# A recurrence beside attention: a quarter of its units moved behind attention, and the end of a sequence laid over the next projections

## The chip, the cores and the metric

The kernel runs on one core of one Trainium2 chip. Its time is the device time of one execution in microseconds (us). One launch computes two layers for 8 sequences of 512 tokens with 256 features, all in float32.

## The reference

Two layers, each `x = x + s * silu(g)`, with `s` from a recurrent branch and `g` from a second branch, both of the layer-normed input. The first layer (a gated scan, and experts chosen per token) is not touched. The second one is:

```python
# recurrent branch (16 channels a head, 16 heads; x is the normed input)
dx = shift(x) - x;  lerpx = x + dx * xw
r, k, v, g = [(x + dx * lora(lerpx, ...)) @ W.T for each]      # lora: l + tanh(z @ a.T) @ b.T
w = exp(-exp(lora(x + dx * lora(lerpx, d...), d...)))
for t in range(T):                                             # state: 16 x 16 a head
    y[t] = r[t] @ (state + u * outer(k[t], v[t]))
    state = w[t] * state + outer(k[t], v[t])
s = (silu(g) * layernorm_per_head(y)) @ oW.T
# second branch
x2 = xn + causal_attention(rmsnorm(xn))                        # 16 heads, rotated queries, one shared latent key
f = x2 + shared_expert(rmsnorm(x2)) + top2_of_8_experts(rmsnorm(x2))
out = x + s * silu(f)
```

## The kernel before

Three phases follow each other; the change is in the third, `phase_c`, which takes the sequences one by one (B = 8) in a loop on every engine. Each engine has its own instruction list; the order in a list is the order of the code, and engines meet only at semaphores. Nothing plans the order, it is written out.

One sequence has these stages.

- Projections (TensorE L1080 `product`, in the order of the table `PRE`): la (the low-rank inputs), lb (their outputs, one pair for each of d, r, k, v, g), pr (the projections), then xb, ckv and q0 to q7. VectorE makes each mix from lb (L1509), GpSimd adds x to it (L1742), TensorE projects it. VectorE and GpSimd rotate ckv and the eight q (L1523, L1524, L1747, L1749). ScalarE copies r, k, v, g out of PSUM and makes w (L1343, L1359).
- Attention, 32 steps of two heads and 128 queries each (8 head pairs, 4 query tiles, step i has tile i % 4), written in one loop per engine. TensorE: `scores` (L1124, L1127), then `turn_probs` for step i-2 (L1139); `weigh_values` (L1165) and `spread_inverse` (L1156) every 8 steps. VectorE: `highest` (the row maxima, L1545). ScalarE: `exp` (L1372) and `keep` (L1381), the copy of the transposed probabilities. Scores are two steps ahead (LAG = 2).
- The recurrence runs beside attention in 32 units (one unit: 8 heads x 16 channels of k on the partitions, for one channel of v). SP copies one channel of v over 16 partitions a head (L1048, 256 KB, four buffers), VectorE multiplies by k (`outer`, L1558) and scans over time with w (`scan`, L1565), GpSimd sets the first column of the state (L1753) and multiplies with r (`product`, L1758), TensorE sums over channels in bank 4 for four units at a time (`reduce_state`, L1147). One unit stands in each step of VectorE's loop: `highest(i)`, `scan(i)`, `outer(i + 1)`. Sixteen units make one half of y (`read_out`, L1570).
- Behind attention (TensorE L1249 `result` for all that follows): mean0, wo0, wo1 (the output of attention), mean1, var0; VectorE adds wo to xn (L1598), subtracts the means (L1593); ScalarE squares (L1405); the root (L1779), the scaled rows xb (L1605), their transposes xc0, xc1 (L1086), the copy of the first (L1614), var1, and the gate.
- Experts, e = 0 to 8: TensorE `up(e)`, `down(e - 1)`; ScalarE silu (L1400), VectorE `hidden` (L1660) and four accumulations (L1703). Between two experts VectorE does one step each of the two halves of y's normalisation (reciprocal L1666, L1670, L1674, L1679) and of the next sequence's head (gate, sum, statistics, norm, rms, lerp; L1439 to L1481).
- End of a sequence: the gate matmuls o0 and o1 (8 matmuls), silu of the accumulator (L1424), product (L1709) and sum (L1713), store. The next sequence's first projection waits for PSUM reads of this one, and the loop jumps here.

PSUM has eight banks of 128 x 512 float32. `Outputs` gives each result of the tables `PRE` and `POST` its bank in turn, all eight, and TensorE waits before it writes for the reader of the result that had the bank before.

## Time and profile before

| | us |
|---|---|
| three runs | 2812.10, 2814.43, 2822.92 (median 2814.43) |
| profiled execution | 2821.07 |
| its span, first to last instruction | 2818.8 |
| TensorE (PE) busy | 2332.4 (83%), 9640 records |
| VectorE (DVE) busy | 1768.5 (63%) |
| GpSimd (POOL) busy | 1029.7 (37%) |
| ScalarE (ACT) busy | 924.0 (33%) |
| mean granted TensorE clock | 0.887 |

Busy shares are means over stages that have different limits, so they say little here; phase_c has one period per sequence, and the windows of one period are what to read. A group of instructions is shown by its line, engine and operation, with its count, busy time and mean duration, and the idle time of the engine just ahead of it with what ended that (`<-`). A float32 matmul leaves two records. "issue" is idle time for which the profile shows no releaser. PEclk is the granted clock as a share of 2.4 GHz; 0.5 is 1.2 GHz.

### The profile page before, as it was taken

The page shows a single profiled execution, that of the slowest core. Times are in us where ns is not written, and L with a number is a line of the kernel's source. Part 1 is how long each engine was busy: PE and PEld are TensorE (multiplying, and loading weights), DVE is VectorE, ACT ScalarE, POOL GpSimd, SP SyncE. Part 2 cuts the span into 40 slices and gives each one's busy share as a digit, 9 for nine tenths or more (in the row PEclk, how much of TensorE's full clock was granted, in tenths as well). Part 3 has the DMA queues.
Part 4 walks back from the last instruction along what each step waited for, and adds up shares of the span by engine and source line. Part 5 has one row for each costly group of instructions (what it writes and reads, how often), then busy time and mean ns, then how long its engine had stood idle before and what let it go on. Part 6 is the DMA issues. An engine that isn't in the chain of part 4 may idle for free.

```text
span 2818.8 us, 36206 instructions
## 1 busy us (share of the span) xinstructions
PE 2332.4 (83%) x9640; PEld 1276.8 (45%) x9641; DVE 1768.5 (63%) x2977; ACT 924.0 (33%) x2467; POOL 1029.7 (37%) x986
## 2 busy tenths in 40 slices
PE   7887599996877987798789778978888797789778
PEld 3443366664434533443454345434534443454345
DVE  5777344443278658666855785477748566855777
ACT  2333123321235224412532352234225413522352
POOL 2113200001166146506622661265155416622661
PEclk9998799998778997898789888979997898889799
DMA  4341401003043014202410440143024203401430
GB/s 138 112 143 63 152 26 30 28 28 98 4 55 62 23 24 72 57 9 33 77 34 9 50 70 23 21 57 67 9 29 76 47 9 41 78 24 19 55 71 16
DMA packets 100043, 143.57 MB, mean 51 GB/s; under 512 B 7953, under 2 KB 61841, under 8 KB 99857
## 3 DMA queue, kind: packets, MB, share of 16 engines
q1 hardware_dynamic: 92370, 128.18, 23.1%
q0 software_dynamic: 3264, 8.93, 1.1%
q10 hardware_dynamic: 4224, 4.19, 0.4%
q8 instruction: 91, 1.49, 0.2%
q14 instruction: 94, 0.77, 0.1%
HBM read 50.94 MB, written 23.24 MB: 26 GB/s over the span
## 4 chain that ended last, share of the span: by engine, by line
issue 29%; PE 16%; DMA 11%; DVE 9%; POOL 8%; ACT 2%; DVEq 0%; POOLq 0%; ACTq 0%
DMA arena<-arena 11%; PE bank L1249 8%; DVE arena L1565 3%; POOL arena L1742 3%; POOL arena L1747 2%; DVE arena L1545 2%; PE bank L1139 2%; DVE arena L1558 2%; PE bank L1124 2%; PE bank L1165 2%; POOL arena L1749 1%; ACT arena L1372 1%; PE bank L1156 1%; ACT arena L1381 1%; PE bank L1147 1%
## 5 line engine op out<-in xcount | busy, mean ns | idle before, releaser
L1249 PE MATMUL bank<-arena 128*128 128x256 f32 (+2 forms) x1728 | 531.8, 468 | 6.4 <-DVE arena L1574 6.2
L1758 POOL TENSOR_TENSOR arena<-arena 128x512 f32<-128x512 f32 x256 | 370.1, 1446 | 291.7 <-issue 151.8
L1080 PE MATMUL bank<-arena 128*128 128x512 f32 (+2 forms) x896 | 423.9, 619 | 46.1 <-issue 18.6
L1372 ACT ACTIVATE arena<-bank,arena 128x128 f32<-128x128 f32 (+3 forms) x512 | 267.0, 526 | 545.5 <-DVE arena L1545 488.7
L1139 PE MATMUL bank<-arena 128*128 128x128 f32 x1280 | 257.4, 340 | 208.9 <-ACT arena L1381 207.5
L1249 PEld LDWEIGHTS bank<-arena 128*128 128x128 f32 x1728 | 331.8, 201 | 196.9 <-issue 153.3
L1565 DVE TENSOR_TENSOR_SCAN arena<-arena 128x512 f32<-128x512 f32 x256 | 375.8, 1468 | 0.0
L1139 PEld LDWEIGHTS bank<-arena 128*128 128x128 f32 x1280 | 186.2, 175 | 249.0 <-ACT arena L1372 213.5
L1080 PEld LDWEIGHTS bank<-arena 128*128 128x128 f32 (+2 forms) x896 | 159.7, 189 | 296.3 <-issue 255.4
L1124 PE MATMUL bank<-arena 64*128 64x128 f32 (+3 forms) x1024 | 257.3, 586 | 43.9 <-DVE arena L1524 26.9
L1558 DVE TENSOR_TENSOR arena<-arena 128x512 f32<-128x512 f32 x256 | 209.1, 817 | 77.0 <-DMA arena<-arena 76.7
L1545 DVE TENSOR_REDUCE arena<-bank 128x2 f32<-128x256 f32 (+3 forms) x256 | 209.3, 817 | 53.3 <-PE bank L1127 52.9
L263 PE MATMUL bank<-arena 128*128 128x512 f32 x384 | 189.4, 647 | 34.3 <-DVE arena L417 18.1
L1381 ACT ACTIVATE arena<-bank 128x128 f32<-128x128 f32 (+3 forms) x512 | 196.7, 441 | 11.6 <-PE bank L1139 11.4
L1742 POOL TENSOR_TENSOR arena<-arena 128x512 f32<-128x512 f32 x80 | 99.3, 1268 | 250.8 <-DVE arena L1509 250.8
L1753 POOL COPY arena<-arena 128x1 f32<-128x1 f32 x256 | 164.1, 641 | 0.0
L1124 PEld LDWEIGHTS bank<-arena 64*128 64x128 f32 x1024 | 95.7, 229 | 141.2 <-issue 95.8
L1509 DVE SCALAR_TENSOR_TENSOR arena<-bank,arena 128x512 f32<-128x512 f32 x80 | 60.2, 753 | 157.8 <-PE bank L1080 152.7
L696 PE MATMUL bank<-arena 128*128 x624 | 147.3, 388 | 1.3 <-ACT arena L730 1.3
L676 PE MATMUL bank<-arena 128*128 x312 | 142.1, 598 | 1.2 <-DVE arena L771 1.2
L817 POOL TENSOR_TENSOR arena<-arena 128x1 f32<-128x1 f32 x39 | 21.2, 543 | 330.6 <-DVE arena L763 330.6
L263 PEld LDWEIGHTS bank<-arena 128*128 128x128 f32 x384 | 76.0, 204 | 130.8 <-issue 90.2
(189 smaller groups left out, 2887.4 us busy)
## 6 DMA issues: line engine op xcount, KB each, us to landing
arena<-arena SPq DMA_DIRECT2D x256, 256.0 KB
arena<-in_L_attn_h SPq DMA_DIRECT2D x17, 512.0 KB, 3.6
arena<-in_W1T SPq DMA_DIRECT2D x8, 1024.0 KB, 5.8
arena<-in_W2T SPq DMA_DIRECT2D x8, 1024.0 KB, 8.8
sorted_rows<-arena SPq DMA_DIRECT2D x42, 128.5 KB, 9.0
arena<-sorted_rows SPq DMA_DIRECT2D x40, 128.5 KB, 2.1
gate_rows<-arena SPq DMA_DIRECT2D x39, 128.0 KB, 1.7
arena<-s_rows SPq DMA_DIRECT2D x9, 512.0 KB, 4.6
```

Of the source, the lines that this page charges most:

```text
L263: last = nc.tensor.matmul(bank[s + q][:, :], gru_w[layer][:, k, q * D + m * P:q * D + (m + 1) * P], src[:, k, :], start=(k == 0), stop=(k ...
L1080: last = nc.tensor.matmul(dst[0:rows, 0:width], w, x, start=(n == 0), stop=(n == len(pairs) - 1))
L1124: nc.tensor.matmul(bank[2 * (i % LAG) + half][:, 0:n], qT[rows, p, qt * P:(qt + 1) * P], ckvT[rows, 0:n], start=True, stop=False)
L1139: last = nc.tensor.transpose(bank[5 + half][:, kt * P:(kt + 1) * P], probs[s % PROBS][:, kt * P:(kt + 1) * P], ident)
L1249: last = nc.tensor.matmul(dst[o], w, x, start=first, stop=last_one)
L1372: nc.scalar.activation(probs[s % PROBS][:, 0:n], bank[2 * (i % LAG) + half][:, 0:n], ACT.Exp, bias=neg_max[:, s:s + 1], accum_out=row_sum[ ...
L1381: nc.scalar.activation(turned[h % HGROUP][:, 0:qt + 1, qt * P:(qt + 1) * P], bank[5 + half][:, 0:(qt + 1) * P].rearrange("p (k c) -> p k c ...
L1545: nc.vector.tensor_reduce(neg_max[:, 2 * i:2 * i + 2], psum[:, at:at + 1024].rearrange("p (h k) -> p h k", h=2)[:, :, 0:n], X, ALU.max, ne ...
L1558: nc.vector.tensor_tensor(kv[n % 2], copies[n % COPIES], proj["k"][:, n // HD, :], ALU.mult).then_inc(kv_done, 1)
L1565: nc.vector.tensor_tensor_scan(state[n % 2][:, 1:T + 1], proj["w"][:, m, :], kv[n % 2], VEC["init"][:, m * HD + j:m * HD + j + 1], ALU.mul ...
L1742: nc.gpsimd.tensor_tensor(mix[n % 2][:, m, :], mix[n % 2][:, m, :], xnT[:, m, :], ALU.add).then_inc(mixed, 1)
L1758: nc.gpsimd.tensor_tensor(prods[n % PRODS], state[n % 2][:, 0:T], proj["r"][:, m, :], ALU.mult).then_inc(prod_done, 1)
```

## The change

- Each of the 32 units is no longer tied to a step. Unit 0 runs in the projections (between the rotations of q5 and q6), units 1 to 23 in those steps of attention with i % 4 != 3, units 24 and 25 behind the last maximum, 26 and 27 between the steps up to the gate, 28 to 31 between experts 0 to 3.
- So the second half of y is complete only in the experts. Its mean and variance, and the reductions, use bank 4 alone (`LAST_BANK`), which both tables leave out: each now turns over seven banks. Its reciprocal, scale, affine and gate, the gate matmuls (`gates`), product, sum and store run in the next sequence's projections.
- The loop on each engine is turned: `before_attention(0)`, then seven times `attention(b)` and `before_attention(b + 1)`, then `attention(B - 1)` and an end of its own. The head that was made for a ninth sequence is gone.
- State has four buffers, not two. Its first column is no longer written by GpSimd but by a small DMA of SP per unit. The load of the next sequence stands within SP's copies, after the 28th.
- xb, xbT, acc and y have memory of their own; the wait for the store moves from the first rotation to the first accumulation.
- Ahead of the last weighing of values TensorE does mean0 and six of the 16 wo matmuls. Scores no longer wait for the last rotated q as a whole.

The core of the diff:

```diff
+STATES = 4
+UNIT_STEP = [i for i in range(PSTEPS) if i % NT != NT - 1]
+EARLY = len(UNIT_STEP)
+PRE_BANKS = [3, 5, 6, 7, 0, 1, 2]
+POST_BANKS = [2, 0, 1, 3, 5, 6, 7]
+LAST_BANK = 4
 # SP
+            def first_column(b, n):
+                if n >= STATES:
+                    sp.wait_ge(prod_done, UNITS * b + n - STATES + 1)
+                sp.dma_start(state[n % STATES][:, 0:1], VEC["init"][:, n:n + 1]).then_inc(init_in[n % STATES], 16)
+            def sequence(b, last):
                 sp.wait_ge(a_read, pre.read(b, "pr_v1"))
+                for n in range(STATES):
+                    first_column(b, n)
                 for n in range(UNITS):
+                    copy_value(b, n)
+                    if n > STATES:
+                        first_column(b, n - 1)
+                    if n == EARLY + COPIES and not last:
+                        sp.wait_ge(pv_mm, GROUPS * b + 2 * GROUPS)
+                        load_sequence(b + 1)
+                first_column(b, UNITS - 1)
+                store_sequence(b)
 # TensorE, projections
                 project(b, "r")
                 lora_b(b, "v", "v", th[1])
+                if ended is not None:
+                    gates(ended, 0)
                 project(b, "k")
                 lora_b(b, "g", "g", th[1])
+                if ended is not None:
+                    gates(ended, 1)
 # TensorE, attention
+                    if i == PSTEPS + LAG:
+                        pe.wait_ge(y_read, 2 * b + 1)
+                        pe.wait_ge(s_exp, STEPS * b + STEPS)
+                        result("mean0", [(full, mean_m, y[:, 0, :], True, True)], bank[post.bank("mean0")])
+                        pe.wait_ge(y_out, GROUPS * b + GROUPS - 1)
+                        wo(0, 0, range(GROUPS - 1))
+                        wo(1, 0, range(GROUPS - 1))
 # TensorE, experts
+                    if e == 2:
+                        reduce_state(b, EARLY // 4)
+                    elif e == 6:
+                        reduce_state(b, EARLY // 4 + 1)
+                    elif e == ME:
+                        mean_last(b)
                     if e:
                         down(e - 1)
-                pe.wait_ge(o_done, 2 * b + 2)
-                for half in range(2):
-                    by_tokens(f"o{half}", ...)
+                var_last(b)
 # ScalarE, end of the experts
                 nc.scalar.activation(acc, acc, ACT.Silu).then_inc(f_done, 1)
+                root_last(b)
 # VectorE
+            def unit(b, n):
+                scan(b, n)
+                if n + 1 < UNITS:
+                    outer(b, n + 1)
 # VectorE, projections, after the mixes of x
+                        if x == "d":
+                            ln_inv(ended, 1)
+                        elif x == "r":
+                            ln_scale(ended, 1)
+                            ln_affine(ended, 1)
+                            ln_gate(ended, 1)
+                        elif x == "v":
+                            gate_rows(ended, 0)
+                        elif x == "g":
+                            gate_rows(ended, 1)
+                            residual(ended)
+                        if name == "q5":
+                            outer(b, 0)
+                            v.wait_ge(w_step, 2 * b + 2)
+                            scan(b, 0)
+                            outer(b, 1)
 # VectorE, attention
-                    if i < PSTEPS:
-                        scan(i)
-                    if i + 1 < PSTEPS:
-                        outer(i + 1)
+                    if i in UNIT_STEP and i > 0:
+                        unit(b, UNIT_STEP.index(i))
+                    if i == PSTEPS:
+                        unit(b, EARLY)
+                    if i == PSTEPS + 2:
+                        unit(b, EARLY + 1)
+                        center()
 # VectorE, between the experts
+                    if e < 4:
+                        unit(b, EARLY + 4 + e)
+                    elif e == 4:
+                        ln_inv(b, 0)
+                    elif e == 5:
+                        read_out(b, 1)
+                        ln_scale(b, 0)
+                    elif e == 6:
+                        ln_affine(b, 0)
+                    elif e == 7:
+                        center_last(b)
+                        ln_gate(b, 0)
 # GpSimd, the product of a unit
-                    nc.gpsimd.tensor_copy(state[n % 2][:, 0:1], VEC["init"][:, m * HD + j:m * HD + j + 1]).then_inc(init_set, 1)
-                    g.wait_ge(init_set, UNITS * b + (n + 1))
+                    g.wait_ge(init_in[n % STATES], 16 * (UNITS // STATES) * b + 16 * (n // STATES + 1))
                     g.wait_ge(scan_done, UNITS * b + (n + 1))
```

`mean_last`, `var_last` and `gates` are TensorE's matmuls in bank 4; `center_last` and `root_last` are VectorE's subtraction and ScalarE's root for the second half of y.

## Rows read from the trace of the kernel before

**Rows 1.** Windows of one sequence (length; busy us and records an engine; clock, DMA).
```profile
2040.00:2103.20 63.20, 55.12 (x128) 21.99 (x128) 26.08 (x46) 13.01 (x21) 29.77 (x26) 0.97 0.18 26
2103.20:2211.40 108.20, 82.77 (x514) 43.75 (x514) 94.42 (x103) 55.44 (x185) 72.78 (x69) 0.81 0.43 69
2211.40:2223.50 12.10, 9.05 (x62) 4.78 (x62) 2.13 (x4) 4.68 (x11) 3.43 (x3) 0.72 0.04 11
2223.50:2238.30 14.80, 10.72 (x47) 8.10 (x48) 6.50 (x12) 1.81 (x8) 4.76 (x7) 1.00 0.18 63
2238.30:2299.40 61.10, 58.84 (x188) 35.71 (x186) 44.47 (x99) 14.20 (x27) 4.66 (x5) 0.92 0.03 10
```

**Rows 2.** Groups of instructions by line, of attention (2103.2 to 2211.4).
```profile
L1565 DVE TENSOR_TENSOR_SCAN arena<-arena 128x512 f32<-128x512 f32 x32 | 47.8, 1493 | 0.0
L1372 ACT ACTIVATE arena<-bank,arena 128x128 f32<-128x128 f32 (+3 forms) x62 | 32.0, 521 | 65.0 <-DVE arena L1545 58.0 <-PE bank L1139 6.9
L1545 DVE TENSOR_REDUCE arena<-bank 128x2 f32<-128x256 f32 (+3 forms) x32 | 26.2, 818 | 6.1 <-PE bank L1127 6.0
L1558 DVE TENSOR_TENSOR arena<-arena 128x512 f32<-128x512 f32 x32 | 25.6, 800 | 7.7 <-DMA arena<-arena 7.7
L1753 POOL COPY arena<-arena 128x1 f32<-128x1 f32 x32 | 20.5, 640 | 0.0
```

**Rows 3.** Windows: first four copies of v, then three parts of attention.
```profile
2074.00:2098.50 24.50, 23.44 (x66) 10.67 (x65) 13.07 (x26) 6.01 (x10) 12.81 (x12) 1.00 0.39 43
2104.50:2126.50 22.00, 16.25 (x72) 8.03 (x71) 20.46 (x21) 10.77 (x38) 16.64 (x16) 0.61 0.44 51
2126.50:2146.00 19.50, 14.90 (x88) 7.19 (x87) 11.48 (x15) 7.63 (x25) 8.93 (x11) 0.65 0.46 75
2146.00:2204.50 58.50, 45.23 (x321) 25.78 (x320) 54.28 (x60) 33.47 (x110) 40.79 (x37) 0.91 0.47 81
```

**Rows 4.** Instructions of two lines in attention (ns: least, median, most).
```profile
L1565 DVE TENSOR_TENSOR_SCAN arena<-arena x32: 1194/1277/1964, 2104.8 to 2211.3; 128x512 f32<-128x512 f32 x32
...
L1558 DVE TENSOR_TENSOR arena<-arena x32: 660/667/1509, 2103.0 to 2209.6; 128x512 f32<-128x512 f32 x32
```

**Rows 5.** DMA issues of the whole execution (count, KB each, us to landing).
```profile
arena<-in_gate_b SPq DMA_DIRECT2D x1, 4.0 KB, 6.5
```

**Rows 6.** Timeline behind the last maximum (start, us, engine, line; idle before).
```profile
2224.23 9.75 PE L1249 MATMUL bank<-arena 128*128 128x512 f32 x38 [0.78 <-DVE arena L1574]
...
2238.03 0.75 DVE L1614 TENSOR_SCALAR arena<-bank,arena 128x512 f32<-128x512 f32 x1
```

**Rows 7.** Timeline of the experts, from TensorE's, ScalarE's and VectorE's lists.
```profile
2238.27 52.59 PE L1249 MATMUL bank<-arena 128*128 128x512 f32 x154
...
2239.22 1.28 ACT L1410 ACT_TABLE_LOAD   x1
...
2255.53 3.34 DVE L1666 RECIPROCAL arena<-arena 128x512 f32<-128x512 f32 x1
...
2285.97 0.69 DVE L1660 TENSOR_TENSOR arena<-arena,bank 128x512 f32<-128x512 f32 x1 [2.34 <-ACT arena L1400]
```

**Rows 8.** TensorE's timeline from one sequence's last expert to the next scores.
```profile
2033.33 5.35 PE L1249 MATMUL bank<-arena 128*128 128x256 f32 x24
2040.12 0.69 PE L1080 MATMUL bank<-arena 128*128 128x512 f32 x1 [1.45 <-DVE arena L1703]
2042.90 6.83 PE L1080 MATMUL bank<-arena 128*128 128x512 f32 x11 [2.08 <-issue]
...
2054.95 24.11 PE L1080 MATMUL bank<-arena 128*64 128x512 f32 x52 [0.83 <-POOL arena L1742]
...
2103.27 0.49 PE L1124 MATMUL bank<-arena 64*128 64x128 f32 x4 [3.36 <-DVE arena L1524]
```

**Rows 9.** VectorE's timeline at the end of the last sequence.
```profile
2810.22 1.41 DVE L1703 SCALAR_TENSOR_TENSOR arena<-bank,arena 128x256 f32<-128x256 f32 x4
...
2814.17 1.23 DVE L1713 TENSOR_TENSOR arena<-arena 128x1024 f32<-128x1024 f32 x1
```

More of the change, by code:

```diff
@@ L942, in phase_c @@
         kv = [mem.take(T) for _ in range(2)]
-        state = [mem.take(T + 1) for _ in range(2)]
+        state = [mem.take(T + 1) for _ in range(STATES)]
         probs_at = mem.at
@@ L1230, in _, with attention, result, by_tokens @@
                         product(b, name, [(spread, bonus[:, i, :])])
-                pe.wait_ge(a_read, pre.read(b, "lat"))
-                pe.wait_ge(v_read, pre.read(b, "q7"))
+            def attention(b, final):
+                full = slice(None), slice(0, T)
+                def result(name, pairs, dst):
+                    begin(b, name, post, post_read)
+                    for n, (o, w, x, first, last_one) in enumerate(pairs):
+                        last = nc.tensor.matmul(dst[o], w, x, start=first, stop=last_one)
+                    last.then_inc(made2, 1)
+                def by_tokens(name, tiles, lhs, rhs, n):
+                    result(name, [((slice(None), slice((i % 2) * D, (i % 2 + 1) * D)), lhs(i, c), rhs(c), c == 0, c == n - 1)
+                                  for i in tiles for c in range(n)], bank[post.bank(name)])
+                def wo(half, odd, groups):
+                    dst = bank[post.bank(f"wo{half}")]
+                    i = 2 * half + odd
+                    for c in groups:
+                        last = nc.tensor.matmul(dst[:, odd * D:(odd + 1) * D], yT[c][:, i * P:(i + 1) * P], wo_w[:, c, :],
+                                                start=(c == 0), stop=(c == GROUPS - 1))
+                    if odd:
+                        last.then_inc(made2, 1)
                 for i in range(PSTEPS + LAG + 3):
@@ L1325, in _ @@
             act.sem_inc(a_read, 1)
[L1326 removed]
+            act.sem_inc(a_read2, 1)
             act.sem_inc(stored, 16)
```

438 lines of the change are left out of this document (242 added, 196 removed).

## The prediction

> **What bounds the kernel now.** I read the windows of one sequence first. The eight sequences of the last phase repeat every 259.4 us: 63.2 us of projections, 108.2 us of attention with the recurrence beside it, 12.1 us until its last value, 14.8 us up to the gate, 61.1 us of experts with the gated output [rows 1]. TensorE is busy for all but about 2 us of the experts; in attention VectorE leads, 94.4 of 108.2 us. What is worth looking for in each stretch is the engine without gaps.
>
> The groups of attention [rows 2] say what VectorE does there: 32 scans (mean 1493 ns), 32 outer products (800 ns), 32 row maxima (818 ns). ScalarE's exponentials wait 58.0 us for the maxima: VectorE works in order, maximum, scan, outer product, so each exponential queues behind a unit of the recurrence. VectorE itself waits 7.7 us for copies of v and 6.0 us for scores.
>
> The windows inside attention [rows 3] show three rates. In the first 22.0 us VectorE is busy 20.5 at a granted clock of 0.61, in the next 19.5 us only 11.5, in the last 58.5 us 54.3. The middle one is the DMA's: the copies move 51, 75 and 81 GB/s in the three, for 256 KB each 5.1, 3.5 and 3.2 us a copy, against 3.4 us a step (108.2 / 32).
>
> **The change, part by part.** Durations are those of one execution of 2821.1 us (span 2818.8, 2.3 around it); the median of the runs shown is 2814.4, so the result is taken 6.6 lower at the end.
>
> *Attention, eight times.* Of 32 units (a scan and an outer product) unit 0 goes into the projections, 24 to 31 go behind the last maximum; 23 stay. Of VectorE's 94.4 us, 26.2 are maxima and about 5 small work, so a unit costs (94.4 - 31) / 32 = 2.0 us, nine units 18, and 76 us of VectorE's work is left. Idle now: 13.8 us. If that stayed, less the 7.7 of DMA wait, the stretch would take 82 us, 26 less. But the others are near then: per four steps TensorE needs 8.4 us at full clock (82.8 x 0.81 / 8), ScalarE 6.9 (55.4 / 8), VectorE 9.5 after and 11.8 before. Three engines in order, with scores two steps ahead, should leave more gaps; I take 16 us: 76 + 16 = 92. The low end of the gain: the first 22 us at half clock give nothing, the DMA's gap stays, and the other 58.5 us shrink in the ratio 9.5 to 11.8 but lose a fifth of it: 9. I take -16, between -9 and -26, nearer VectorE's rows than TensorE's, since its gaps are the smaller. Eight times: -128.
>
> GpSimd's 32 copies of the first column (20.5 us a sequence) go too [rows 2]. They go at nothing: GpSimd is busy 72.8 of 108.2 us. The 32 DMAs in their place stand in SP's order between the copies of v, and each waits for the product four units back. No row shows a copy of 4 bytes a partition; the nearest, 4 KB, landed 6.5 us after issue in a crowded queue [rows 5]. Four units are 15 us, so a product waits nothing, or 6.5 us once if the queue is full; below nothing it can't go but by a shorter GpSimd. I take 0.
>
> Scans take 1194 to 1964 ns and outer products 660 to 1509 [rows 4]. The Trainium skill's page "SBUF — State Buffer", section "SBUF: two separate sides", says that a VectorE operation with two inputs in SBUF and a GpSimd operation that reads there lock each other out for a whole instruction. The spread of those two rows agrees. By that rule the units carried into the experts, whose products go with them, would all come at the long price: the second rival below.
>
> *Behind the last maximum, eight times.* Units 24 and 25 fall where VectorE is busy 2.1 of 12.1 us [rows 1]: hidden. On TensorE mean0 (0.85) and six of the 16 wo matmuls (0.43 each) move ahead of the last weighing: 3.4 us, of which 0.7 fills a wait, so +2.7; behind it 3.6 less stands in the block of 38 records in 9.75 us [rows 6]: -0.9. Unit 26 stands between the second residual sum and the root; ScalarE's squares there take 1.5 us, the unit 2.0 and some wait: +0.7. Unit 27 stands in the chain from the scaled rows to the copy of their transpose (2238.03) [rows 6], that the gate waits for: +1.7. Together +1.5, between -1 and +4: +12.
>
> *Experts, eight times.* TensorE has 154 records in 52.6 us, almost without a gap [rows 7]. It gets two reductions of 1.04 us and the mean of the second half, 0.85: +2.9, not hidden. VectorE gets units 28 to 31 and loses one reciprocal of 3.34 us and 1.9 us of small steps. An expert takes 5.17 us of TensorE and 2.3 of VectorE's own two steps, so 2.8 are free; experts 1 to 4 bring 3.2 to 3.4. It is some 1.3 us late at the next sequence's normalisation, for which it already waits 2.34 us ahead of L1660 [rows 7], and TensorE after it: +1.5. Together +4.4, between +2.9 and +8: +35.
>
> *From the last expert to the next scores, seven times.* I count from the last expert's 8 records, 2033.33 + 1.8 = 2035.1, to 2103.3 [rows 8]: 68.2 us, of which 19.8 lie before la_dd (2054.95) and 45.0 up to the last projection. Gone: the gate matmuls ahead (3.5), the wait for the last accumulate behind them, and the pause of 2.08 us after the first record, which I read as the loop's jump. It comes back at the head of attention, in place of the 3.36 us for the last rotated q [rows 8]. Then la_dd comes at 17.1: lerp 3.3 (its chain is 0.7 longer), two thirds of the first projections wait for the accumulate until 5.0, then 11.3 of la, tanh, lora and mix as now, and 0.4 for two more table loads of 1.28 us [rows 7]; 0.4 less since the tanh comes earlier. Behind it 45.0, the eight gate matmuls 3.5, less 1.9 of gaps that they fill, and 1.6 because the reciprocal (3.34) stands between the d and r mixes and project r waits for r: 48.2. Then the jump 2.1, and 0.4 for units 0 and 1 among the rotations. In sum 67.8: -0.4, between -3 and +4: -2.
>
> *The end, once.* The last sequence's second half has nothing to run beside: root with load 1.9, reciprocal 3.3, three steps 1.9, gates 3, product and sum 1.9, waits 1.8: 13.8, where 3.8 stand now (2811.6 to 2815.4) [rows 9]. The dropped ninth head gives 2.5 back: +7.5, between +4 and +12.
>
> Sum: -128 + 12 + 35 - 2 + 7.5 = -75.5: 2746, by the median 2740 us.
>
> **Rivals.** *The copies set the pace.* Four of them queued at once moved 43 GB/s over 24.5 us [rows 3], about 5.3 us a copy. For it: the DMA share is 0.44 to 0.47 in all of attention and no higher where the rate is, as if full. Needed after: 23 copies in 92 us, 4.0 each. If they stay at 5.3, the lead of six copies lasts to about unit 14; ten more units then cost 1.4 each: the gain of attention is 2 and not 16: -16 + 52.5 = +36, 2851. It decides where a copy takes over 4.0 us to the end. Against: the rate rises from 51 to 81 within a sequence, and the demand falls.
>
> *The experts pay it back.* The units come there at the long price of rows 4, 3.5 us and not 2.0, since GpSimd's products run beside: 6 us a sequence, all of it TensorE's: 48, so 2788. For it: GpSimd has 4.7 us of work in that stretch now and gets about 6 more. Against: VectorE's result for the next matmul is up to 3.8 us ahead, which takes part of it.
>
> *TensorE is attention's true bound.* Clock 0.81, busy 82.8 of 108.2 [rows 1]: the gain is 7, the costs the same: -56 + 52.5: 2811, no change. Against: 58.5 us with VectorE 93% busy at clock 0.91 [rows 3].
>
> *It overlaps better*: idle stays near 6 us, 82 us of attention: 80 less, 2660.
>
> **Chances.** The forecast with its own 2700 to 2785: 0.60; the experts pay back 0.12; TensorE 0.09; the copies 0.09; better overlap 0.10. A difference under 0.5% (14 us; 2800 to 2828) can't be told from none here. Faster are the forecast, the payback and the better one, 0.82, less 0.03 for the payback's tail: 0.79; same 0.09; slower, the copies and that tail, 0.12. The range leaves out the end of the better case and most of the copies: 2675 to 2815.
>
> **What would show it.** A period near 250 us. From the first score to the last maximum near 92 us with VectorE busy near 76, and little wait for copies; if that wait is over 15 us a sequence, the copies rule. The experts near 57 us for 52.6, with longer gaps before L1660's successor. The first projections without the 2.08 us pause, the reciprocal behind the d mixes, five table loads a sequence for three. I am wrong if attention stays above 100 us, or if TensorE's gaps in the experts pass 8 us a sequence.

## The result and the profile after

The changed kernel takes 2926.36 us (median of 4 runs, 2916.67 to 2935.75) against 2813.26 for the kernel before: a ratio of 1.040, interval 1.035 to 1.046, some 113 us slower. The forecast was 2740, faster. The profiled execution has a span of 2933.9 us; it had 2818.8.

The windows of one sequence, the same five stretches as in [rows 1] and with the same columns:
```profile
2092.60:2159.80 67.20, 62.46 (x146) 25.81 (x147) 34.64 (x52) 15.50 (x23) 27.49 (x22) 0.92 0.17 25
2159.80:2277.50 117.70, 80.85 (x499) 44.48 (x498) 77.02 (x94) 55.63 (x185) 48.03 (x34) 0.81 0.45 49
2277.50:2292.20 14.70, 11.38 (x76) 6.88 (x76) 5.59 (x7) 4.68 (x11) 5.64 (x5) 0.88 0.48 54
2292.20:2305.40 13.20, 7.44 (x31) 5.67 (x30) 8.61 (x14) 3.78 (x11) 4.49 (x6) 0.83 0.61 132
2305.40:2364.50 59.10, 57.05 (x186) 32.76 (x186) 43.44 (x95) 10.83 (x23) 11.49 (x10) 0.92 0.07 14
```
The whole loss of attention is in the second row: 117.7 us where 108.2 stood, although VectorE's work fell from 94.4 to 77.0 as forecast. All engines have gaps now, and the DMA moves 49 GB/s instead of 69 at the same share. The row above it is longer too (67.2 against 63.2), the row of the experts is shorter because the gated output has gone from it into the next sequence's first row.

The groups of the page that answer to [rows 2], for the whole execution (busy and mean ns, idle before them):
```profile
L1885 POOL TENSOR_TENSOR arena<-arena 128x512 f32<-128x512 f32 x256 | 361.6, 1413 | 794.8 <-DVE arena L1639 446.3
...
L1619 DVE TENSOR_REDUCE arena<-bank 128x2 f32<-128x256 f32 (+3 forms) x256 | 206.5, 820 | 160.3 <-PE bank L1147 142.8
L1632 DVE TENSOR_TENSOR arena<-arena 128x512 f32<-128x512 f32 x256 | 199.7, 780 | 168.4 <-DMA arena<-arena 168.2
```
The outer products (L1632) wait 168.2 us for copies of v, where the page of before has 76.7. The products (L1885) wait 341.8 us for the small DMAs (L1059), as the third view below says. It and the two ahead of it give the durations of SyncE's issues in ns (least, median, most): first the copies of the kernel before, then the copies and the small DMAs of the one after.
```profile
L1048 SPq DMA_DIRECT2D arena<-arena x256: 647/1464/4796, 768.5 to 2717.0; - x128
```
```profile
L1052 SPq DMA_DIRECT2D arena<-arena x256: 647/4312/4777, 768.8 to 2849.8; - x128
```
```profile
L1059 SPq DMA_DIRECT2D arena<-arena x256: 521/577/5014, 766.1 to 2855.6; - x128
...
  POOL arena L1885: 341.8, 108
```
A copy's issue took 1.5 us in the median, up to 4.8, and takes 4.3 in the median now. SyncE's own list, in attention (start, duration):
```profile
2182.29 0.58 SPq L1059 DMA_DIRECT2D arena<-arena  x1
2183.27 4.10 SPq L1052 DMA_DIRECT2D arena<-arena  x1
2187.42 0.58 SPq L1059 DMA_DIRECT2D arena<-arena  x1
2188.11 4.23 SPq L1052 DMA_DIRECT2D arena<-arena  x1
```
Copy and small DMA take turns almost without a pause: 4.0 to 4.5 us, then 0.6 to 0.9, about 5.1 us a pair. They do so from 2183.3 on, to the end of the stretch, 94 of its 117.7 us. SyncE, which no row ahead of the prediction times, holds back the rest there.

To compare stages over all sequences I took from VectorE's timeline the first and last row maximum, the last scaled value and the accumulates of the experts. Mean of the first seven sequences, us:

| stretch | before | after | forecast of the difference |
|---|---|---|---|
| first to last row maximum | 109.6 | 108.9 | -16 |
| to the last value | 12.8 | 15.4 | +1.5 with the next row |
| to the first accumulate | 29.0 | 27.9 | |
| first to last accumulate | 44.6 | 48.8 | +4.4 |
| to the next first maximum | 64.6 | 73.1 | -0.4 |
| period | 260.7 | 274.0 | -10.5 |

The table counts from maximum to maximum, the forecast from the first score. By the forecast's count attention went from 108.1 to 117.9 us in the sequence of the rows, and in the mean from 110.7 to 118.0 (+7.3): the first maximum now comes 9.8 us after the first score in that sequence, where it came 1.2 after. From the last accumulate to the next first score the mean went from 63.4 to 63.9 (+0.5). The experts and the stretch behind the last maximum came out as forecast, and the way to the next scores within the range given for it; attention did not.

### The profile page after: what moved, and what is told of

Read it like the earlier page. It is cut to its first block, busy times and chain, and to the rows that moved or that the text cites. A ratio compares the mean times of both kernels' runs of the same rounds, so it can differ in the third digit from the quotient of the medians.

```text
span 2933.9 us, 35683 instructions
## 1 busy us (share of the span) xinstructions
PE 2356.5 (80%) x9632; PEld 1285.1 (44%) x9633; DVE 1736.5 (59%) x2951; ACT 932.3 (32%) x2466; POOL 892.0 (30%) x722
## 3 DMA queue, kind: packets, MB, share of 16 engines
q1 hardware_dynamic: 128178, 127.28, 27.6%
## 4 chain that ended last, share of the span: by engine, by line
PE 30%; DMA 19%; issue 10%; DVE 9%; POOL 3%; ACT 3%; SPq 1%; DVEq 0%; ACTq 0%; POOLq 0%
DMA arena<-arena 19%; PE bank L1272 13%; PE bank L1098 10%; PE bank L1161 1%; DVE arena L1619 1%; DVE arena L1632 1%; DVE arena L1639 1%; PE bank L1216 1%; PE bank L1144 1%; ACT arena L1442 1%; POOL arena L1872 1%; DVE arena L1825 1%; POOL arena L1874 1%; DVE arena L1689 1%; PE bank L1171 1%
## 5 line engine op out<-in xcount | busy, mean ns | idle before, releaser
L1885 POOL TENSOR_TENSOR arena<-arena 128x512 f32<-128x512 f32 x256 | 361.6, 1413 | 794.8 <-DVE arena L1639 446.3
L1098 PE MATMUL bank<-arena 128*128 128x512 f32 (+2 forms) x896 | 448.3, 649 | 39.4 <-ACT arena L1403 22.2
L1272 PE MATMUL bank<-arena 128*128 128x512 f32 (+2 forms) x1312 | 447.0, 496 | 6.3 <-ACT arena L1407 6.3
L1639 DVE TENSOR_TENSOR_SCAN arena<-arena 128x512 f32<-128x512 f32 x256 | 341.5, 1334 | 23.3 <-issue 22.9
L1272 PEld LDWEIGHTS bank<-arena 128*128 128x128 f32 x1312 | 256.1, 209 | 192.0 <-issue 155.3
L1161 PEld LDWEIGHTS bank<-arena 128*128 128x128 f32 x1280 | 188.0, 177 | 282.6 <-ACT arena L1442 254.0
L1144 PE MATMUL bank<-arena 64*128 64x128 f32 (+3 forms) x1024 | 245.0, 561 | 70.4 <-ACT arena L1442 69.1
L1632 DVE TENSOR_TENSOR arena<-arena 128x512 f32<-128x512 f32 x256 | 199.7, 780 | 168.4 <-DMA arena<-arena 168.2
L1098 PEld LDWEIGHTS bank<-arena 128*128 128x128 f32 (+2 forms) x896 | 167.4, 197 | 301.1 <-issue 236.2
L1867 POOL TENSOR_TENSOR arena<-arena 128x512 f32<-128x512 f32 x80 | 103.2, 1307 | 224.0 <-DVE arena L1664 224.0
L263 PEld LDWEIGHTS bank<-arena 128*128 128x128 f32 x384 | 75.1, 202 | 129.6 <-issue 88.9
L1403 ACT ACTIVATE arena<-bank 128x512 f32<-128x512 f32 (+1 forms) x96 | 55.6, 595 | 233.9 <-PE bank L1098 233.8
L696 PEld LDWEIGHTS bank<-arena 128*128 128x128 f32 x624 | 116.0, 191 | 29.9 <-issue 14.3
```

Source lines behind the costliest of these rows:

```text
L263: last = nc.tensor.matmul(bank[s + q][:, :], gru_w[layer][:, k, q * D + m * P:q * D + (m + 1) * P], src[:, k, :], start=(k == 0), stop=(k ...
L696: last = nc.tensor.matmul(out_bank[u % 2][:, 0:D], hT[:, c, :], w2s[:, bass.ds((E - 1) * FC * D + c * D - e * (FC * D), D)], start=False, ...
L1098: last = nc.tensor.matmul(dst[0:rows, 0:width], w, x, start=(n == 0), stop=(n == len(pairs) - 1))
L1144: nc.tensor.matmul(bank[2 * (i % LAG) + half][:, 0:n], qT[rows, p, qt * P:(qt + 1) * P], ckvT[rows, 0:n], start=True, stop=False)
L1161: last = nc.tensor.transpose(bank[5 + half][:, kt * P:(kt + 1) * P], probs[s % PROBS][:, kt * P:(kt + 1) * P], ident)
L1272: last = nc.tensor.matmul(dst[o], w, x, start=first, stop=last_one)
```

## The experiments

Every kernel was compared with runs of the kernel before on the same chip (medians 2810 to 2815); the ratios carry the comparisons, and 0.01 is 28 us. "After" and "before" below are the two kernels.

**Who writes the first column.** GpSimd's copy of 128 x 1, as before, in place of SyncE's DMAs; the four state tiles and the moved units stay.
```
-                for n in range(STATES):
-                    first_column(b, n)
...
+                    nc.gpsimd.tensor_copy(state[n % STATES][:, 0:1], VEC["init"][:, n:n + 1]).then_inc(init_set, 1)
```


> The changed kernel, with the first column of the state written by GpSimd again (four buffers stay) and SP's 32 small DMAs a sequence gone. Theory: the small DMAs hold the copies of v (SP issues each only after a product, in order with the copies, and a product waits for them 341.8 us in all), so products no longer wait for a DMA, the outer product's wait of 168 us falls under 60, and attention goes from 118 to about 100 us a sequence: 2780 to 2810 us. Rival: the copies themselves are slow because they queue on the DMA engines, whatever stands between them: the outer product's wait stays over 130 us and the time at 2890 or more.

Measured: 2836.0 us, ratio 1.007 (1.004 to 1.010). 94 of the 113 us are gone with the small DMAs, but it is not the 2780 to 2810 that I expected. The outer products wait 0.0 us for copies, and the median issue of a copy is near the least one:
```profile
L1052 SPq DMA_DIRECT2D arena<-arena x256: 647/662/4796, 766.3 to 2750.1; - x128
```

The reverse, the small DMAs put into the kernel before (with four state tiles):
```
+                    if n > STATES:
+                        first_column(b, n - 1)
```


> The kernel before, with only this part of the change: four state buffers, and the first column of each unit by a small DMA of SP in the order of the change, not by GpSimd. Theory (the small DMAs hold the copies): attention with all 32 units becomes bound by the copies at about 5 us each, 150 us for 108: over 3000 us, at the least 2900. Rival (the copies are slow for another reason, such as the pace at which units are asked for): within 30 us of the kernel before.

Measured: 3120.6 us, ratio 1.108 (1.102 to 1.114). Attention alone takes 148.2 us from the first to the last maximum, where it took 109.6: with 32 units it needs some 29 pairs of issue at 5.1 us. So the small DMAs cost more in the kernel with more units in attention, 309 us, and the two runs show the same pace.

**Why they cost: a wait, a DMA or its packets.** On top of GpSimd's column, first SyncE's 28 waits without the DMAs, then the 32 DMAs without the waits, into memory that nobody reads, then the same DMAs with one row of 32 bytes in place of 128 rows of 4.
```
+            def column_wait(b, n):
+                if n >= STATES:
+                    sp.wait_ge(prod_done, UNITS * b + n - STATES + 1)
...
```


> The kernel after, with the first column written by GpSimd as in the pool-column run (2836 us), but SyncE still waits at the 28 old places of each sequence for the product four units back; no small DMA is issued. If it is SyncE's order (a copy held behind a wait for a product) that costs the 90 us between 2836 and 2926, this run comes near 2926. If it is the DMAs themselves (their issue and their place in the rings beside the copies), it stays near 2836. I expect 2840, within 2825 to 2860: the product four units back is some 12 us old when its place in the order comes.

Measured: 2841.8 us, ratio 1.009 (1.006 to 1.012), against 1.007 without them: the waits cost nothing that can be told.
```
+            def unread_column(b, n):
...
+                sp.dma_start(nobody[:, n:n + 1], VEC["init"][:, n:n + 1]).then_inc(unread, 16)
```


> The kernel after, with the first column written by GpSimd, but SyncE issues a DMA of the same shape (128 partitions, 4 bytes each) at each of the 32 old places, into memory that nobody reads, with no wait for a product ahead of it. If the DMAs themselves cost the time (they fill the queue in which the copies stand, so each copy lands later), this comes to 2890 to 2930 with VectorE's outer products waiting for copies again. If the wait of a product for its column was the cost, or SyncE's waits, it stays near 2836. I expect 2905.

Measured: 2922.3 us, ratio 1.039 (1.035 to 1.042), the time of after. No product waits for these DMAs, so it isn't the products' wait either. (SyncE itself waits once a sequence, ahead of the last one, until the others have landed.)
```
-                sp.dma_start(nobody[:, n:n + 1], VEC["init"][:, n:n + 1]).then_inc(unread, 16)
+                sp.dma_start(nobody[0:1, 8 * n:8 * n + 8], VEC["init"][0:1, 0:8]).then_inc(unread, 16)
```


> As the run with the 32 unread DMAs a sequence (2922 us), but each moves one row of 32 bytes in one partition, not 4 bytes in each of 128. If the number of small transfers inside a DMA costs the time (128 each, beside the copies' own 128), this comes near the kernel without small DMAs, 2836 to 2850. If each DMA costs by its issue on SyncE or its place in the queue, whatever is in it, it stays near 2922. I expect 2850.

Measured: 2925.3 us, ratio 1.039 (1.035 to 1.042). My expectation was wrong: a DMA of one row costs what one of 128 rows costs. Its issue on SyncE is no shorter (least, median, most ns):
```profile
L1061 SPq DMA_DIRECT2D arena<-arena x256: 670/722/4712, 768.1 to 2851.1; - x128
```
So with either content it is the further DMA in the order that costs. Nor are its packets the cost: the queue moved 95410 packets in this execution and 128178 in the one ahead of it.

**The same DMAs from another engine.** ScalarE issues them behind each pair of exponentials.
```
                         exp(2 * i + 1)
...
+                        act.dma_start(nobody[:, i:i + 1], VEC["init"][:, i:i + 1]).then_inc(unread, 16)
```


> The changed kernel with GpSimd's column (2836 us) and 32 unread DMAs of 128 x 4 bytes a sequence, now issued by ScalarE behind each pair of exponentials, in a queue of their own. If the cost in SyncE's queue (2922) was its order of issue, where copy and small DMA take turns at 5.1 us a pair, the copies run free here, and only ScalarE's issue costs: 2840 to 2860. If the small DMAs hold up the engines wherever they are queued, 2900 or more. I expect 2850.

Measured: 3018.6 us, ratio 1.072 (1.067 to 1.077), wrong again. The copies do run free (their issue, first row, and VectorE waits 0.0 us for them), but the small DMAs now hold up ScalarE (second row), and the exponentials stand behind it:
```profile
L1054 SPq DMA_DIRECT2D arena<-arena x256: 647/662/4789, 766.3 to 2934.8; - x128
```
```profile
L1462 ACTq DMA_DIRECT2D arena<-arena x256: 513/1072/4279, 799.5 to 2912.6; - x128
```
An issue that takes 0.5 us at least takes 1.07 in the median and up to 4.28 while copies are under way from the other queue. Of the 183 us over 2836, 19.3 are the run's own doing: ahead of its last DMA of a sequence ScalarE waits for the landing of the others. The page "DMA: Bandwidth & Descriptors" of the Trainium skill says, in "Issuing engines are not separate DMA queues", that DMAs of all issuers run on the same engines, and that issuing from several saves only the issuer's time. The trace fits the first part; the issuer's time, which that text calls usually small beside the DMA itself, is here most of the cost.

**Why attention had nothing to give.** In the kernel before, scan, outer product and product of every fourth unit cut to 8 columns, with nothing put elsewhere:
```
+def wide_of(n):
+    return 8 if n % 4 == 3 else T
```


> The kernel before with scan, outer product and product of every fourth unit (8 of 32, at the steps that the changed kernel leaves free) cut to 8 of 512 columns: that part of the recurrence isn't computed; the copies, waits and every other instruction stay. It prices alone what attention gains when VectorE has eight units less, with nothing put elsewhere. By the forecast's term (16 us a sequence for nine units) 14 us a sequence go: 2700. If attention is bound by the copies' rate or by TensorE and ScalarE behind one another, 3 to 7 us a sequence: 2755 to 2790. I expect 2740.

Measured: 2810.7 us, ratio 1.000 (0.998 to 1.003). A quarter of the recurrence's work on VectorE is gone and no time with it, where I expected 2740. This is the run that the forecast's main term needed and did not have. Its row of attention, counted from the first maximum (columns as in [rows 1]; before has 107.0 us by this count), and its groups of maxima and outer products in the whole execution:
```profile
2083.20:2189.80 106.60, 81.61 (x506) 44.37 (x504) 78.71 (x103) 55.88 (x185) 55.21 (x68) 0.81 0.44 70
```
```profile
L1551 DVE TENSOR_REDUCE arena<-bank 128x2 f32<-128x256 f32 (+3 forms) x256 | 209.7, 819 | 126.3 <-PE bank L1133 126.2
...
L1564 DVE TENSOR_TENSOR arena<-arena 128x512 f32<-128x512 f32 (+1 forms) x256 | 184.2, 720 | 103.6 <-DMA arena<-arena 103.0
```
VectorE is busy 78.7 us of 106.6, about what it is in the changed kernel. What it lost in work it now waits: 126.2 us for scores in the execution, where before had 52.9, and 103.0 for copies, where it had 76.7.

Copies of v cut to 8 of 512 columns, alone and with the thin units:
```
-                    sp.dma_start(copies[n % COPIES],
+                    sp.dma_start(copies[n % COPIES][:, 0:8],
```


> The kernel before with every copy of v cut to its first 8 of 512 columns, in the same 128 rows; outer products read what lay in the rest, so the recurrence isn't computed rightly, but every instruction stays. It takes the load off the DMA queue. VectorE's 76.7 us of waits for copies go; if the copies pace attention, 60 us or more come back: 2750 or less. If TensorE's chain is as near a bound, half or less of it: 2780 to 2800. I expect 2775.

> The kernel before with thin copies and, besides, the 8 units of 32 cut to 8 columns on VectorE and GpSimd (what both leave out is as in those two runs). If VectorE was the bound once the copies are out of the way, this run lies 60 us or more below the thin copies alone. If the chain scores, maximum, exponential, transpose is the bound, it lies within 25 us of it. I expect 20 below it.

Measured: 2757.3 us, ratio 0.979 (0.972 to 0.986), and 2738.8, ratio 0.974 (0.969 to 0.979). Their rows of attention:
```profile
2067.40:2170.60 103.20, 81.14 (x506) 44.83 (x504) 93.40 (x103) 56.02 (x185) 74.10 (x68) 0.82 0.02 2
```
```profile
2044.80:2145.10 100.30, 79.95 (x506) 43.07 (x504) 76.93 (x103) 56.00 (x185) 56.30 (x68) 0.83 0.02 2
```
Without the copies' load attention takes 103.2 us, and eight units less then bring 3 more (16 to 19 us in the execution). In the last row VectorE is busy 76.9 us of 100.3 and the DMA moves 2 GB/s, and still the stretch is 100 us long. Neither VectorE's work nor the copies fill it; that scores, maxima, exponentials and transposes behind one another do is what is left to argue, since 24 of 32 units still stand between the maxima and no run takes them out. The forecast's 92, counted from the first score, lay below it.

**The loops' jumps.** In after, VectorE's loop begins anew between the last rotated q and the first maximum. Its seven iterations written out, in after, in after with GpSimd's column, and as the control in before:
```
-            with v.Fori(0, B - 1) as b:
+            for b in range(B - 1):
```


> The changed kernel, with VectorE's seven loop iterations written out one behind the other, so VectorE has no jump between projections and attention. Theory: the pauses of 2.9 us before and 3.8 us behind the first two maxima of a sequence are the jump, now exposed at the head of attention: about 5 us a sequence back, 2880 to 2895 us. Rival: the copies set the pace of attention and swallow it: 2915 to 2930, the pauses gone all the same. A third way: the pauses stay, being no jump.

> The kernel after with GpSimd's column and VectorE's seven iterations written out instead of a loop. Theory: at the head of attention VectorE pauses 2.9 and 3.8 us where its loop begins anew, on the path to the first exponentials, in seven sequences; without the pauses 3 to 6 us a sequence go: 2795 to 2815. Rival: the first scores wait for the rotated q and the steps behind are TensorE's, so it stays at 2836.

> The kernel before with VectorE's loop over the eight sequences written out, nothing else. It is the control for the unrolled run of the changed kernel (2801 us): there the loop's jump stood at the head of attention, here it stands between the last accumulate and the first projections. If the jump is hidden there, 2811 and no change, and then the moved units with GpSimd's column are worth 10 us in all. If this run gains as much as the changed kernel did by it (34 us, 2780), the move itself is a loss of 20. I expect 2807.

Measured: 2918.8 us, ratio 1.039 (1.033 to 1.045); 2801.5, ratio 0.996 (0.994 to 0.999); 2790.1, ratio 0.991 (0.988 to 0.995). With the small DMAs the jump is hidden behind them. Without them it brings 30 us in the changed kernel and, against my expectation, 25 in the kernel before. In both changed kernels the pauses of VectorE at the head of attention are gone. All four loops (TensorE, ScalarE, VectorE, GpSimd) written out:

> The changed kernel with GpSimd's column and the seven iterations of the last phase written out on TensorE, ScalarE, VectorE and GpSimd (with VectorE's alone: 2801 us). TensorE's jump stands at the head of attention, where its first scores wait for the rotated q as well. If the jump of TensorE was the later of the two, 8 to 15 us go: 2788. If it was hidden behind the rotations, 2801 stays. I expect 2793.

> The kernel before with the eight iterations of the last phase written out on TensorE, ScalarE, VectorE and GpSimd (VectorE's alone: 2790 us). TensorE's pause of 2.08 us at the first projection goes too: by the forecast's reading of it 8 to 17 us less, 2775 to 2782. If VectorE's jump was the later one, 2790 stays. I expect 2778. Against the changed kernel with the same two mendings (2797) it then shows the move to lose some 19 us.

Measured: 2796.8 us, ratio 0.995 (0.993 to 0.998), and 2767.9, ratio 0.984 (0.980 to 0.988). The last is the fastest kernel of this study that computes everything, 5.4% below after and 1.6% below before, and has nothing of the change in it. Against one another the two show the rest of the change, without small DMAs and without jumps: 0.0115, some 32 us slower. I call them the clean pair, and the rest "the move".

**Where the moved units cost.** Unit 0 out of the rotations and into step 0 of attention, in after and in the unrolled kernel with GpSimd's column:
```
-                        if name == "q5":
-                            outer(b, 0)
...
-                    if i in UNIT_STEP and i > 0:
+                    if i in UNIT_STEP:
```


> The changed kernel, with unit 0 (outer product, scan, second outer product) no longer between the rotations of q5 and q6: the first outer product comes behind the last rotation, the unit in step 0 behind the first maximum. Theory: the first maximum comes about 3.5 us earlier and attention's end follows it, 20 to 30 us in all: 2895 to 2905. Rival: the recurrence loses its head start and the copies set the pace, so nothing or a loss of up to 30: 2920 to 2955.

> The kernel after with GpSimd's column, VectorE's loop written out, and the inserted unit 0 and outer products moved from between the rotations of q5 and q6 to behind the last rotation and into step 0 of attention. Theory: the inserted work of 5.3 us holds back q6 and q7 and with them the first scores, so the sequence starts earlier than in the unrolled run and the unit is hidden in step 0: 10 to 30 us less than that run: 2780 to 2800, the first below the kernel before. Rival: attention's first four steps are already VectorE's, and the unit costs there what it cost ahead: the same as the unrolled run.

Measured: 2936.4 us, ratio 1.044 (1.038 to 1.051), and 2824.0, ratio 1.002 (1.000 to 1.004), both against my expectation, the second 16 to 23 us slower than with the unit among the rotations. The unit costs more in attention's first step: 99.7 us between first and last maximum, where 95.1 stood, and only 1.3 less ahead of it. Units 24 to 31 cut to 8 columns:
```
+def wide_of(n):
+    return 8 if n >= 24 else T
```


> The changed kernel with GpSimd's column and VectorE's loop written out (2801 us), and scan, outer product and product of units 24 to 31 cut to 8 of 512 columns: that part of the recurrence isn't computed. It prices what the eight units cost behind the last maximum and in the experts' stretch. By the forecast's terms (1.5 and 1.5 us a sequence of VectorE's lateness) some 20 us go: 2781. If the units cost more there, with GpSimd's products beside VectorE's steps, 40 us or more: 2760 or below. I expect 2775.

Measured: 2780.8 us, ratio 0.987 (0.984 to 0.991): 26 us less by the ratios, 21 by the medians; the expectation was 20 to 26. The traces put it ahead of the experts, not in them: from the last value to the first accumulate 27.1 us became 24.7 in the mean, and the accumulates themselves went from 48.4 to 48.0. Unit 27 behind the copy of the transposed rows instead of ahead of it:
```
-                unit(b, EARLY + 3)
                 v.wait_ge(made2, post.made(b, "xc0"))
...
+                unit(b, EARLY + 3)
```


> The changed kernel with GpSimd's column and all four loops written out (2797 us), and unit 27 moved from ahead of the copy of the transposed rows, which the gate waits for, to behind it. By the forecast's term of 1.7 us a sequence 13 us go, of which VectorE's later routing gives some back: 2788. If the unit only moves the delay from the gate to the routing, 2797 stays.

Measured: 2799.6 us, ratio 0.994 (0.991 to 0.997), no difference from 0.995. The copy comes 0.5 us earlier there, and the routing begins 16.8 us behind the last value in both: at this place the unit held nothing up.

## Why the prediction was wrong

By the ratios the 113 us are: 94 for the small DMAs; 32 for the move itself; and -13, since the jumps cost 33 us in the changed kernel and 45 in the one before.

The 32 come about so in the clean pair's traces, by the forecast's count and as means of seven sequences: attention -7.0, up to the first accumulate +1.6, the accumulates +4.3, from there to the next scores +4.9, so +3.8 a sequence and not -10.5; the rest is the last sequence. Attention gained less than half of the 16, and the way to the next scores, put at -0.4, took most of that back.

**The DMAs of the first column, "I take 0": the step that failed first.** The forecast asked when a product has its column, and took 6.5 us once from the landing of a 4 KB DMA [rows 5]. The product's wait was never the price. Each small DMA is one more issue on SyncE between two copies, and the copies' issue is itself a rate: 5.1 us a pair, 94 us in all. The rival "the copies set the pace" has the right picture (5.3 us a copy, over 4.0 decides, outer products that wait, 2851) and was given 0.09, because it read the pace from the first four copies and saw it rise later [rows 3]. That it would be held down to the end by the very DMAs that the forecast priced at nothing, I did not join up. The DMA's rate beside its share says what happened: 43 GB/s at 0.39 for the first four copies, 81 at 0.47 later in attention [rows 3], and 49 at 0.45 now, so the engines are as busy as late in the old attention and move as little for it as with the first four copies. Those took 5.3 us each with no small DMA between them. My reading is that the small DMAs do not add their own time to a copy's but keep the copies at their slow pace; why a DMA between two copies would do that stays open. The Trainium skill's page "DMA: Bandwidth & Descriptors", section "Rules for kernel authors", says to coalesce many small transfers, which speaks against this edit; the runs with the unread DMAs agree, with 86 to 89 us for 256 of them on SyncE.

**Attention, "I take -16", between -9 and -26.** VectorE's work fell to 77 us as forecast (76). The 16 us of idle time beside it were a guess, and both ends of the range were too hopeful. The thin units price eight units' work: 0 with the copies as they are. With the copies thin as well, 100.3 us are left of the stretch. In the clean pair, counted from first to last maximum, it went from 107.1 to 94.6; but 6.7 us of step 0 lie ahead of the first maximum there, where 1.1 did, so it gained 7.0. That is more than the thin units gave, and the moved units took nine copies out of the stretch with them, which the thin ones left in it; whether that is the difference no run shows. The rival "TensorE is attention's true bound" had the gain at 7 and was given 0.09; its number came out in the clean pair, but no run made TensorE's work less, so its cause is not shown, and the match may be luck. I had argued against it with a stretch where VectorE was 93% busy: a busy engine and a bound are not the same where engines wait for one another in turn.

**From the last expert to the next scores, "-0.4".** The table has +8.5 in this kernel, up to the first maximum. Of that, +0.5 lies ahead of the first score, within the range; 8.0 lie between the first score and the first maximum, where the forecast put nothing more than now, and so lengthen attention. They are the 5.3 us of unit 0 and two outer products among the rotations, priced at 0.4, and the jump. VectorE's list at the head of attention:
```profile
2158.93 1.67 DVE L1632 TENSOR_TENSOR arena<-arena 128x512 f32<-128x512 f32 x1
2160.64 2.00 DVE L1639 TENSOR_TENSOR_SCAN arena<-arena 128x512 f32<-128x512 f32 x1
2162.55 1.68 DVE L1632 TENSOR_TENSOR arena<-arena 128x512 f32<-128x512 f32 x1
2164.16 0.68 DVE L1688 TENSOR_TENSOR arena<-bank,arena 128x512 f32<-128x512 f32 x1
...
2169.59 1.02 DVE L1619 TENSOR_REDUCE arena<-bank 128x2 f32<-128x256 f32 x2 [2.89 <-issue]
2174.46 1.29 DVE L1639 TENSOR_TENSOR_SCAN arena<-arena 128x512 f32<-128x512 f32 x1 [3.84 <-issue]
```
The last two q are rotated behind them, and the maximum waits 2.89 us more for the loop's jump. TensorE has done its first two steps and then stands still for 9.55 us, since the third needs the exponentials:
```profile
2159.80 0.49 PE L1144 MATMUL bank<-arena 64*128 64x128 f32 x4
...
2170.92 1.65 PE L1144 MATMUL bank<-arena 64*128 64x384 f32 x4 [9.55 <-ACT arena L1442]
```
The forecast put the jump of 2.1 us in TensorE's list; it stood in VectorE's, twice (2.89 and 3.84). The same place in the changed kernel with GpSimd's column and the loops written out:
```profile
1812.14 1.60 DVE L1622 TENSOR_TENSOR arena<-arena 128x512 f32<-128x512 f32 x1
1813.85 1.93 DVE L1629 TENSOR_TENSOR_SCAN arena<-arena 128x512 f32<-128x512 f32 x1
1815.70 1.69 DVE L1622 TENSOR_TENSOR arena<-arena 128x512 f32<-128x512 f32 x1
...
1819.76 1.00 DVE L1609 TENSOR_REDUCE arena<-bank 128x2 f32<-128x256 f32 x2
```
Here the unit and its neighbours alone remain: 5.1 us, then the two rotations, then the maximum, 6.7 us behind the first score where 1.1 are in the kernel before with its loops written out. TensorE's part, from the last expert to the next scores, is 71.5 us in this sequence, where 67.8 were forecast:
```profile
2362.61 1.89 PE L1272 MATMUL bank<-arena 128*128 128x256 f32 x8
2365.27 1.13 PE L1209 MATMUL bank<-arena 128*128 128x512 f32 x2 [0.77 <-POOL arena L1918]
2367.87 5.57 PE L1098 MATMUL bank<-arena 128*128 128x512 f32 x12 [1.48 <-DVE arena L1556]
2375.09 21.36 PE L1098 MATMUL bank<-arena 64*128 64x512 f32 x28 [1.65 <-ACT arena L1403]
...
2435.97 0.49 PE L1144 MATMUL bank<-arena 64*128 64x128 f32 x4
```
Waits of 0.77, 1.48 and 1.65 us stand in it. But this is one of the two longest of the seven sequences, which take 66.4 to 71.5 us and 68.6 in the mean, and what differs between them is TensorE's clock. The block of 28 records behind the three waits, here and one sequence earlier (columns as in [rows 1]):
```profile
2375.09:2396.38 21.29, 21.29 (x28) 6.99 (x29) 11.55 (x11) 1.79 (x3) 8.00 (x6) 0.60 0.00 0
2102.27:2120.21 17.94, 17.94 (x28) 5.86 (x28) 11.45 (x11) 1.78 (x3) 7.96 (x6) 0.71 0.00 1
```
The same matmuls take 21.3 us at a granted clock of 0.60 and 17.9 at 0.71: in this block the clock stands at 1.2 GHz for part of the time. The row of this stretch had 0.97 before and has 0.92 now. In the clean pair the way from the last expert's end to the scores is 59.6 us at a clock of 1.00 in the kernel before (its eight gate matmuls lie ahead of it), and 66.5 us at 0.95 or 71.5 at 0.88 in the changed one. By my estimate from these rows (length times what the clock lacks) at most 3.3 or 8.6 us of that are the clock, and 5.6 in the mean of seven, which covers the +4.9 of the clean pair. The forecast had no term for it. What in the new order lets the clock fall there was not tried.

**Behind the last maximum, "+1.5", between -1 and +4.** +2.6 up to the last value, -1.1 behind it: +1.4. The sum is right. Of its parts, unit 27's 1.7 us moved nothing when the unit was put behind the copy, yet 2.4 us of the stretch went when units 24 to 31 were made thin.

**Experts, "+4.4", between +2.9 and +8.** 4.2 measured; the clean pair gives 4.3. The number is right, its split isn't: 1.5 was for VectorE's late units, and making them thin took 0.4 us off the accumulates. The rival "the experts pay it back", with 6 us a sequence from those units, is out. They did not come at the long price (1964 and 1509 ns) at all; unit 28 and the next outer product in the sequence of the rows, and the ones behind them take the same:
```profile
2321.76 1.28 DVE L1639 TENSOR_TENSOR_SCAN arena<-arena 128x512 f32<-128x512 f32 x1
2322.95 0.67 DVE L1632 TENSOR_TENSOR arena<-arena 128x512 f32<-128x512 f32 x1
```

**The end, "+7.5", between +4 and +12.** From the last accumulate to the span's end there were 7.2 us, and there are 20.6: +13.4. The last sequence's accumulates take 43.7 us where the others take 48.8, 5.1 given back where 2.5 were put: +8.3, right in sum. VectorE's last list, to be set beside [rows 9]:
```profile
2911.92 1.41 DVE L1825 SCALAR_TENSOR_TENSOR arena<-bank,arena 128x256 f32<-128x256 f32 x4
...
2916.39 3.35 DVE L1588 RECIPROCAL arena<-arena 128x512 f32<-128x512 f32 x1 [1.58 <-ACT arena L1411]
...
2925.72 0.69 DVE L1607 TENSOR_TENSOR arena<-arena,bank 128x512 f32<-128x512 f32 x1 [3.94 <-PE bank L1216]
2928.56 0.69 DVE L1607 TENSOR_TENSOR arena<-arena,bank 128x512 f32<-128x512 f32 x1 [2.15 <-PE bank L1216]
```
Root, reciprocal and three steps end 8.5 us behind the last accumulate (7.1 and a wait were put); the gates then cost 3.94 and 2.15 us of waiting.

The sum of what was measured: seven periods of +13.4, the last sequence +21.2 and 0.3 ahead of the first: 115.1, the difference of the two spans.

## What to carry to other kernels

Before a small copy is given to the DMA queue, look at how long the issues already there take. A large transfer's issue that lasts longer than its shortest is a sign that the queue holds its issuer up; here each further DMA, of either size tried, then kept the large ones slow. Before work is moved off the busiest engine, make it thin once without putting it anywhere: if the time stays, as here, something else holds the stretch, and that has to be found first. And price a piece of work inserted ahead of a stage's first step at its full length, not at the little that the engine was idle there.

## What the runs showed of the hardware that I had not expected

- The issue of a copy of 256 KB on SyncE took 0.65 us at least and up to 4.8 with others under way. A DMA of 32 bytes in one row was issued in 0.72 us in the median, one of 128 x 4 bytes in 0.58, and both cost the kernel the same (2925 and 2922 us).
- A queue on another engine does not escape it: ScalarE's issues of small DMAs took 0.51 us at least and up to 4.28 beside SyncE's copies.
- The beginning of a new iteration showed as 2.89 and 3.84 us of pause in VectorE's list; both are gone where the loop is written out. Writing out the loops of the last phase took 1.6% off the kernel before (ratio 0.980 to 0.988).
- The share of the DMA engines in attention was 0.43 at 69 GB/s before and 0.45 at 49 after. "Rules for kernel authors" in the Trainium skill's page "DMA: Bandwidth & Descriptors" says that a transfer whose outermost dimension is under 16 stays on at most that many engines; the copies' is 8, and a share of at most 0.48 wherever copies are all that moves fits it. A copy laid out otherwise was not run, so this stays open.
